# The pair swap of the second attention's queries by two transfers within SBUF, and its row scores later in the step

## What is computed

```python
Q = proj(layernorm(x), Wq, bq); K = proj(ctx, Wk, bk); V = proj(ctx, Wv, bv)   # 16 heads of 16
def _rope(x):                                    # x1, x2: even and odd values of a head
    out = stack([x1 * sin - x2 * cos, -x1 * cos - x2 * sin], axis=-1)
scores = einsum("bhqd,bhkd->bhqk", _rope(Q), _rope(K)); scores = where(mask, neg, scores)
p = where(mask, 0, softmax(scores)); out = einsum("bhqk,bhkd->bhqd", p, V)
x = x + tanh(g_xattn[1]) * (out @ Wo.T + bo)
```

## Time and profile before

| | |
|---|---|
| median of 3 runs | 828.55 us (827.16 to 830.46) |
| the profiled execution | 828.7 us, span 826.9 us |
| busy: TensorE, its weight loads | 706.9, 568.9 us |
| busy: VectorE, ScalarE, GpSimd | 459.7, 333.1, 224.2 us |
| second attention | about 377 to 536 us of the span |
| one step of it (n = 9 to 13) | 16.5 us |

### The profile page before, as it was taken

One profiled execution on the slowest core, in us unless ns is written; L12 is line 12 of the kernel. 1 busy time (PEld: TensorE's weight loads), 2 busy tenths in 40 slices (PEclk: granted clock), 3 DMA queues, 4 the chain that ended last, 5 costly groups with the idle time before them and its releaser, 6 DMA issues.

```text
span 826.9 us, 13638 instructions
## 1 busy us (share of the span) xinstructions
PE 706.9 (85%) x5064; PEld 568.9 (69%) x5064; DVE 459.7 (56%) x946; ACT 333.1 (40%) x752; POOL 224.2 (27%) x208
## 2 busy tenths in 40 slices
PE   5789988989988746467689999799997899999998
PEld 4556755768865326345456665599986799999997
DVE  4557765210127382745657645554877778878812
ACT  3435564656641110001244454532325755565510
POOL 6443421000001170013254332100004545455410
PEclk9969999999999855557599999999999999999999
DMA  6655671480000210301434443030000256656413
GB/s 246 186 149 150 158 214 39 167 355 25 0 0 1 102 73 20 100 1 38 119 90 128 112 120 91 8 148 1 2 1 0 77 176 202 233 189 204 154 39 101
DMA packets 61478, 87.20 MB, mean 105 GB/s; under 512 B 17265, under 2 KB 50801, under 8 KB 60401
## 3 DMA queue, kind: packets, MB, share of 16 engines
q1 hardware_dynamic: 61424, 86.49, 33.1%
HBM read 63.54 MB, written 18.73 MB: 99 GB/s over the span
## 4 chain that ended last, share of the span: by engine, by line
PE 72%; DVE 12%; issue 5%; ACT 4%; DMA 4%; SPq 1%; POOL 0%; ACTq 0%; DVEq 0%; POOLq 0%
PE ps L882 70%; DVE keep L1679 2%; PE ps L888 1%; ACT big L654 1%; DVE keep L1688 1%; DMA keep<-in_gates 1%; ACT keep L664 1%; DMA keep<-in_x 1%; DVE keep L1673 1%; DVE keep L1685 1%; DVE mcol L1499 1%; DMA big<-in_wd 1%; DMA k_rows<-klo 1%; DMA m_rows<-big 1%; DVE mcol L1501 1%
## 5 line engine op out<-in xcount | busy, mean ns | idle before, releaser
L882 PE MATMUL ps<-keep 128*128 128x128 bf16 (+8 forms) x531 | 96.2, 312 | 45.3 <-DVE keep L1679 35.6
L882 PEld LDWEIGHTS ps<-keep 128*128 128x128 bf16 (+2 forms) x531 | 50.7, 132 | 75.2 <-DVE keep L1679 46.7
L882 PE MATMUL ps<-thi,whi 128*128 128x256 f32 x256 | 73.7, 288 | 4.7 <-POOL tlo L589 2.1
L882 PE MATMUL ps<-thi,wlo 128*128 128x256 f32 x256 | 72.4, 283 | 0.0
L882 PE MATMUL ps<-tlo,whi 128*128 128x256 f32 x256 | 72.4, 283 | 0.0
L743 ACT ACTIVATE ps<-ps 128x256 f32<-128x256 f32 x128 | 47.6, 372 | 38.5 <-PE ps L882 38.5
L882 PE MATMUL ps<-qpair,kpair 98*77 98x256 f32 x256 | 59.3, 348 | 3.3 <-ACT big L654 2.2
L490 POOL TENSOR_TENSOR kbr<-khi,keep 128x616 fp32r<-128x616 f32 x32 | 41.3, 1313 | 64.0 <-PE ps L882 64.0
L795 ACT ACTIVATE att<-ps 128x512 f32<-128x512 f32 x48 | 28.6, 595 | 68.4 <-PE ps L882 68.1
L882 PEld LDWEIGHTS ps<-thi,whi 128*128 128x128 f32 x256 | 49.0, 191 | 6.8 <-issue 4.7
L882 PE MATMUL ps<-xhi,phi 128*128 128x512 f32 x128 | 50.7, 396 | 2.8 <-ACT ps L743 2.8
(11 more groups left out here) (216 smaller groups left out, 1862.1 us busy)
## 6 DMA issues: line engine op xcount, KB each, us to landing
qpair<-q_rows SPq DMA_DIRECT2D x16, 768.0 KB, 5.7
q_rows<-qhi SPq DMA_DIRECT2D x32, 256.0 KB, 2.5
big<-in_piw SPq DMA_DIRECT2D x4, 2048.0 KB, 12.4
q_rows<-qlo SPq DMA_DIRECT2D x16, 256.0 KB, 2.4
att<-in_wg SPq DMA_DIRECT2D x8, 512.0 KB, 3.7
att<-in_wu SPq DMA_DIRECT2D x8, 512.0 KB, 4.6
att<-in_wd SPq DMA_DIRECT2D x8, 512.0 KB, 5.5
big<-in_wg SPq DMA_DIRECT2D x8, 512.0 KB, 3.8
```

The lines of the kernel that those rows point to most:

```text
L882: return pe.matmul(out, lhsT, rhs, start=start, stop=stop, skip_group_check=True)
```

## The change

In the second attention the swap is no longer a product. ScalarE, once its own raw queries are written, issues two transfers within SBUF that put the odd partitions of `qraw` on the even ones of a new tile `qswap` and the reverse, 64 partitions of 2 KB each. VectorE's `rotary_b` reads `qswap` instead of PSUM, once both have landed. `project_out` waits for the raw queries alone, since nothing is written to the bank any more.

TensorE's order in the second attention changes as well: `first_rows` comes behind `weigh_values(n, 0)`, `second_rows` behind the last key scores, `weigh_values(n, 1)` right after it, then the maxima, and the transposes last. ScalarE copies the maxima before `copy_xt`. The first attention is as it was.

```diff
@@ -142,6 +142,7 @@
         qhi = [rounded(f"qhi{j}", "big", 2464 + 512 * j, 512).rearrange("p (g q) -> p g q", g=2) for j in range(2)]
         qlo = [rounded(f"qlo{j}", "big", 3488 + 512 * j, 512).rearrange("p (g q) -> p g q", g=2) for j in range(2)]
         xn2 = big(2 * 2 * D, XN2_AT).rearrange("p (s t d) -> p s t d", s=2, d=D)
+        qswap = big(2 * S, XN2_AT).rearrange("p (g q) -> p g q", g=2)
         mrow = big(2 * S, MT_AT).rearrange("p (s q) -> p s q", s=2)
         mcol = [rounded(f"mcol{j}", "big", MAX_AT + 32 * j, 32).rearrange("p (t h) -> p t h", t=2) for j in range(2)]
         qpair = [rounded(f"qpair{j}", "big", QPAIR_AT + 2048 * j, 2048).rearrange("p (t q) -> p t q", t=PAIRS)
@@ -253,7 +254,7 @@
         k_mulA, k_mulB, k_sum, khi_done, klo_done = (sem("k_mulA"), sem("k_mulB"), sem("k_sum"), sem("khi_done"),
                                                      sem("klo_done"))
         v_ps, v_raw, v_done = sem("v_ps"), sem("v_raw"), sem("v_done")
-        q_ps, q_raw, q_perm, q_mulA, q_mulB, q_sum = (sem("q_ps"), sem("q_raw"), sem("q_perm"), sem("q_mulA"),
+        q_ps, q_raw, q_swap, q_mulA, q_mulB, q_sum = (sem("q_ps"), sem("q_raw"), sem("q_swap"), sem("q_mulA"),
                                                       sem("q_mulB"), sem("q_sum"))
         qhi_done, qlo_done = sem("qhi_done"), sem("qlo_done")
         kbr_done, row_ps, max_done = sem("kbr_done"), sem("row_ps"), sem("max_done")
@@ -638,6 +639,11 @@
                                          bias=bq[:, g:g + 1], scale=1.0)
                 ins.then_inc(q_raw, 1)
 
+            def swap_queries(m):
+                act.wait_ge(q_raw, m - B + 1)
+                for a in range(2):
+                    act.dma_start(qswap[1 - a::2], qraw[a::2]).then_inc(q_swap, 16)
+
             def maxima_out(m):
                 act.wait_ge(mT_ps, m + 1)
                 if m >= 2:
@@ -678,6 +684,7 @@
                             high_queries(n + 2)
                         else:
                             raw_queries(n + 2)
+                            swap_queries(n + 2)
                     exponentials(n, (2, 3, 4, 5))
                     if n == 2 * B - 1:
                         round_shared(1)
@@ -685,11 +692,13 @@
                         high_queries(n + 2)
                     invert(n, 0)
                     exponentials(n, (6, 7))
+                    if n + 2 < hi and layer == 1:
+                        maxima_out(n + 2)
                     if n + 3 < hi:
                         copy_xt(n + 3)
                     if n - 2 >= lo and layer == 0:
                         round_xt(n - 2, R_BANK + 1)
-                    if n + 2 < hi:
+                    if n + 2 < hi and layer == 0:
                         maxima_out(n + 2)
                     if n == 2 * B - 1:
                         round_shared(2)
@@ -779,9 +788,11 @@
             act.activation(outp, ps[:, 5, 0:D], ACT.Copy).then_inc(op_copied, 1)
             copy_xt(8)
             raw_queries(8)
+            swap_queries(8)
             copy_xt(9)
             high_queries(8)
             raw_queries(9)
+            swap_queries(9)
             high_queries(9)
             maxima_out(8)
             copy_xt(10)
@@ -906,19 +917,13 @@
                                  c == 0, c == DC - 1)
                 ins.then_inc(q_ps, 1)
 
-            def swap_pairs(m):
-                pe.wait_ge(q_raw, m - B + 1)
-                for g in range(2):
-                    ins = mm(ps[:, m_bank(m), S * g:S * g + S], perm, qraw[:, g, :])
-                ins.then_inc(q_perm, 1)
-
             def project_out(n):
                 pe.wait_ge(attn_done, 2 * n + 2)
                 end = B * (n // B + 1)
                 if n < B:
                     pe.wait_ge(qlo_done, min(n + 4, end))
                 else:
-                    pe.wait_ge(q_mulB, min(n + 4, end) - B)
+                    pe.wait_ge(q_raw, min(n + 4, end) - B)
                 pe.wait_ge(mT_done, min(n + 3, end))
                 for t in range(2):
                     for c in range(DC):
@@ -1004,25 +1009,28 @@
                     if m < hi:
                         project_q(m)
                     key_scores(n, (2, 3))
-                    if m < hi:
-                        if layer == 0:
-                            if m >= 5:
-                                pe.wait_ge(xlo_done, m - 4)
-                            first_rows(m)
-                        else:
-                            swap_pairs(m)
+                    if m < hi and layer == 0:
+                        if m >= 5:
+                            pe.wait_ge(xlo_done, m - 4)
+                        first_rows(m)
                     key_scores(n, (4, 5))
                     if n > lo:
                         project_out(n - 1)
-                    if m < hi:
-                        if layer == 0:
-                            second_rows(m)
-                        else:
-                            first_rows(m)
+                    if m < hi and layer == 0:
+                        second_rows(m)
                     weigh_values(n, 0)
                     if m < hi and layer == 1:
-                        second_rows(m)
+                        first_rows(m)
                     key_scores(n, (6, 7))
+                    if layer == 1:
+                        if m < hi:
+                            second_rows(m)
+                        weigh_values(n, 1)
+                        if m < hi:
+                            maxima_to_rows(m)
+                        if n + 3 < hi:
+                            transpose_xn(n + 3)
+                        continue
                     if n + 3 < hi:
                         pe.wait_ge(max_done, 2 * n + 6)
                         transpose_xn(n + 3)
@@ -1215,13 +1223,11 @@
             project_q(8)
             transpose_xn(9)
             project_q(9)
-            swap_pairs(8)
             for b in range(4, B):
                 output_row(b)
             pe.wait_ge(prepared, 6)
             pe.wait_ge(xt_done, 10)
             first_rows(8)
-            swap_pairs(9)
             second_rows(8)
             maxima_to_rows(8)
             transpose_xn(10)
@@ -1475,11 +1481,11 @@
                 ins.then_inc(qlo_done, 1)
 
             def rotary_b(m):
-                dve.wait_ge(q_perm, m - B + 1)
+                dve.wait_ge(q_swap, 32 * (m - B + 1))
                 if m > B:
                     dve.wait_ge(qlo_done, m)
                     dve.wait_ge(qhi_done, 2 * m)
-                dve.tensor_tensor(qrope, ps[:, m_bank(m), :].rearrange("p (g q) -> p g q", g=2),
+                dve.tensor_tensor(qrope, qswap,
                                   ropeB.unsqueeze(1).to_broadcast([P, 2, S]), ALU.mult).then_inc(q_mulB, 1)
                 dve.wait_ge(q_mulA, m - B + 1)
                 dve.wait_ge(q_mulB, m - B + 1)
```

## The result

The changed kernel takes 840.53 us (median, 838.42 to 841.3), the kernel before, run beside it, 829.5 us (827.16 to 830.79). The ratio is 1.0119, with a 95% interval of 1.0089 to 1.0148. The forecast was 829.0 and its range ended at 834.0: the change is slower, and beyond the range.

The account below looks back on a forecast made before the run. TensorE was taken to bound the step. Steps 9 to 13 at +0.24 us each (+1.2), first step -0.6, start -0.5 and step 14 +0.4 summed to +0.5 us; the forecast was written as 829.0 us, range 823.5 to 834.

Parts of the forecast that it names:

- The rotation's length: Second attention, step 10: from rotary_b to the first row scores stays 2.50 us, as before the change.
- The slack of 0.9: Step 10: queries ready at 451.0, row scores due at 451.90, so the swap's latency is hidden with 0.9 us left.
- ScalarE's issue time: Steps 9 to 13: two issues of 0.36 and 0.42 us delay ScalarE's exponentials, making each step 0.24 us longer.
- a cheap issue: Rival: issues hardly hold ScalarE, steps 0.41 to 0.56 us shorter, 825.4 to 824.7; chance 0.17 together with covered maxima, 820.5.
- The landing: The swap's 128 KB transfer lands 2.2 us after its issue; in step 8 the second issue is 0.45 later.
- what would show it: Signs at step 10: TensorE idle about 1 us before pair 4, VectorE idle before rotary_b, step of 16.6 to 16.9 us.
- The second rival: At rotary_b's wait: the swap lands late and the first row scores wait; 835.5 us at 4.0 us landing; chance 0.18.
- The maxima: Steps 9 to 13: the maxima wait moves to before the second row scores, 0.7 us; moved parts together give 0.
- First step: Step 8: weigh_values fills TensorE's wait for the queries, so step 9 starts at 425.0 instead of 425.6, -0.6 us.
- start: Start of the second attention: TensorE reaches the row scores at 387.65 instead of 388.26; -0.5 us.
- Step 14: ScalarE bounds this step, and maxima_out of query 15 now stands right before its first work: +0.4 us.
- The rival with a chance of 0.06: Before project_q(9): a new idle stretch brings the granted clock's fall forward to 382, giving 833.5 us; chance 0.06.

Follow-up runs that it names:

- e11: Changed kernel with SyncE issuing the two transfers and GpSimd making the keys' block and bias first, run a second time: 825.8 us, ratio 0.9948.
- e8: Changed kernel with ScalarE's copy of the transposed rows for query 9 ahead of the first two transfers: 836.57 us, ratio 1.009.
- e9: Changed kernel with the old swap products put back on TensorE between key scores 3 and 4, read by nobody: 838.76 us, ratio 1.0108.
- e4: Kernel before, swap still a product, with only the change's new order of TensorE's and ScalarE's work: 832.7 us, ratio 1.0031.
- e6: Kernel before with only GpSimd's order changed, keys' block and bias first in the second attention: 828.89 us, ratio 0.9982.
- e10: Kernel before, swap still a product, with the change's new order and GpSimd's keys' block and bias first: 829.65 us, ratio 1.0003.
- e1: Changed kernel with SyncE instead of ScalarE issuing the two transfers of each swap, ahead of its row stores: 840.06 us, ratio 1.0103.

## Why the prediction was wrong

**The rotation's length is the step that failed.** The prediction said: "From rotary_b to the first row scores it took 2.50 us before", and took that over. It is 4.18 us in step 10 and 4.08 in step 8 (417.80 to 421.88). The change replaces a PSUM operand by an SBUF one, and costs an instruction its independence of GpSimd. Queries that were to be ready 8.9 us into the step were ready at 10.7: 1.68 us by the rotation, 0.2 by its start (6.57 instead of 6.37 us into the step), because the normalisation, longer beside GpSimd as well, ends only then. The slack of 0.9 became a wait of 0.30. With SyncE issuing, or with one transfer, these two hold the step at 17.6.

The Trainium skill states the rule (SBUF — State Buffer, Who interferes with whom): "A DVE instruction with two SBUF inputs contends with a GpSimd instruction that reads SBUF"; DVE is VectorE, and the section calls the port pair that they share an exclusive lock. The trace agrees: 1.70 and 1.58 us beside GpSimd, 0.69 without it, and 0.68 with one operand in PSUM beside GpSimd. It was the rule that spoke against this change, and the prediction did not draw on it.

**ScalarE's issue time was mis-sized.** The prediction took 0.36 and 0.42 us and had 0.61 as the upper bound; measured are 0.61 each, +0.75 us per step up to project_out instead of +0.24. The choice by size and partition count was wrong; the row within SBUF was the one to take. The issues within SBUF of the earlier trace rows, of 64 KB, had 0.61 already. In the steps 9 to 11 its part in the loss is real only in company: without it (SyncE issuing) the step at full clock stays at 17.63, without the slow rotation it makes the 17.2 us step. The argument against a cheap issue, that every issue in the trace holds SyncE over 0.3 us, misread the rows: one in the earlier trace rows takes 0.23.

**The landing was right.** Raw queries are there at 415.15 in step 8 and `rotary_b` starts at 417.80: 2.65 us, as forecast (0.45 and 2.2), though by two errors that cancel: the second issue starts about 0.65 us after the raw queries and lands 2.0 after that. In step 10 VectorE does not stand idle before `rotary_b`, as "what would show it" had it, because the normalisation lasts until 454.16. The second rival, a late landing, did not happen; the change is slower for another reason.

**The maxima were right.** 0.69 us before the second row scores, none before the maxima's transposes. But "copy_xt ends about 0.9 us into the next step ... Hidden, with nothing to spare" looked at TensorE alone. Behind the copy stand ScalarE's invert and VectorE's divide and statistics, 0.54 us later, and that puts the normalisation under GpSimd's products. The order-only run prices it: 1.46 us per step where TensorE waits for it.

**First step and start had the wrong sign.** Step 8: forecast -0.6, measured +1.99, from the rotation (1.6 us longer than assumed) and row scores at half clock (1.07). Start: forecast -0.5, measured +1.78. `project_q` of query 9 starts 1.50 us later against that of query 8 ("1 us later" was the forecast) and takes 1.74 more at half clock; the swap's products that are gone give part of it back. The sum had no term for TensorE's clock. **Step 14** was right: +0.31 for +0.4.

**The clock.** The rival with a chance of 0.06 named this place, and `project_q` of query 9 did run at half clock. But the fall was at 377.2, ahead of the first transfer, and the longer wait before `project_q` of query 9 is not shown to be its cause; that half clock was met there is no success of the rival's mechanism. What rows show at half clock is 1.74 us at the start, 1.15 in step 8 (8.00 from the row scores to the end, against 6.85 in e11; 1.07 of it are the first row scores) and 1.5 in step 12 (18.82, against 17.32 in e8 and e9). From its first rise in step 8 to step 13 the clock never falls in the four traces without transfers (before, e4, e6, e10), though TensorE idles 1.54 us a step in e4; it falls in seven of the nine with transfers, each time inside a wait of 1.4 us or more or within 1.5 us behind one, while most such waits bring no fall. So the falls belong to the loss, but which wait brings one, and how much of the total they make, stays open.

## What to carry to other kernels

Before an operand is moved from PSUM to SBUF, look at what GpSimd does at that time: a chain of VectorE instructions cannot be priced by the durations they had with the old operands. When several engines pass work along, cure two suspects one at a time and then together; if each alone moves the step little and both together much, both are limits. Take such a reading from single steps at one clock: a total can stay the same because the clock fell elsewhere. For a DMA issue take the row with the same kind of source and destination, and count it on an engine that others don't wait for.

## What the runs showed of the hardware that was not expected

- Two issues of transfers within SBUF over 64 strided partitions, 128 KB each, hold the issuing engine 0.51 to 0.74 us each, on ScalarE as on SyncE, while SyncE's 128 KB loads of tables held it 0.36 and 0.42.
- GpSimd and VectorE take turns by whole instructions: in the rotation VectorE's 0.69 us becomes 1.70, GpSimd's 1.33 becomes 1.72, and VectorE's product and sum end 0.54 to 0.56 us after GpSimd's instruction each time.
- The granted clock in the same code differs between traces: `project_q` of query 9 ran at half clock behind 2.06 us of idle time, but also behind 0.69 us (e1), and at full clock behind 0.96 us (e8).
